# The last batch of a fused layer: one output product for both halves, and the experts' products spread over eight PSUM banks

## What is computed

```python
def _moe(x, gate_w, expert_w):
    t = x.reshape(B * S, C)
    logits = t @ gate_w.T
    w, sel = jax.lax.top_k(logits, TOP_K)                 # 2 of 8
    w = jax.nn.softmax(w, axis=1)
    comb = jnp.sum(w[..., None] * jax.nn.one_hot(sel, N_EXPERTS), axis=1)
    out = jnp.zeros_like(t)
    for e in range(N_EXPERTS):
        out = out + comb[:, e, None] * (t @ expert_w[e].T)
    return out.reshape(B, S, C)

h = x + _gqa(_rmsnorm(x, attn_norm_w), wq, wk, wv, wo)    # _gqa ends with out @ wo.T
out = h + _moe(_rmsnorm(h, ffn_norm_w), gate_w, expert_w)
```

## Time and profile before

| | us |
|---|---|
| median of 3 runs | 3667.57 |
| lowest and highest run | 3660.76, 3667.74 |
| the profiled execution's own time | 3655.43 |
| its span in the profile | 3653.7 |
| granted TensorE clock, mean over the span | 0.911 |
| TensorE busy | 3193.2 (87%) |
| VectorE busy | 2187.1 (60%) |
| ScalarE busy | 1428.5 (39%) |
| GpSimd busy | 936.6 (26%) |

### The profile page before, as it was taken

One profiled execution on the slowest core, in us unless ns is written; L12 is line 12 of the kernel. 1 busy time (PEld: TensorE's weight loads), 2 busy tenths in 40 slices (PEclk: granted clock), 3 DMA queues, 4 the chain that ended last, 5 costly groups with the idle time before them and its releaser, 6 DMA issues.

```text
span 3653.7 us, 86956 instructions
## 1 busy us (share of the span) xinstructions
PE 3193.2 (87%) x35518; PEld 2230.1 (61%) x35518; DVE 2187.1 (60%) x4820; ACT 1428.5 (39%) x3328; POOL 936.6 (26%) x851
## 2 busy tenths in 40 slices
PE   5689988888988888898868889776999999999998
PEld 5367665666666666666757767665545555554553
DVE  7566777566678666678346645635435545545444
ACT  1534443444443444344136622134433433333241
POOL 0112221412222512231406536341221231220110
PEclk7898998898998989899679989898989999999999
DMA  6111210411111301211348755384111111111000
GB/s 238 41 36 46 65 44 28 128 32 60 51 52 48 122 20 54 60 51 35 100 151 204 183 157 144 103 285 145 23 43 45 47 35 47 41 30 41 1 18 18
DMA packets 224087, 280.89 MB, mean 77 GB/s; under 512 B 35072, under 2 KB 172464, under 8 KB 223312
## 3 DMA queue, kind: packets, MB, share of 16 engines
q1 hardware_dynamic: 184448, 216.93, 18.4%
q0 software_dynamic: 34896, 54.20, 6.7%
q10 hardware_dynamic: 4352, 4.20, 0.3%
HBM read 184.64 MB, written 90.62 MB: 75 GB/s over the span
## 4 chain that ended last, share of the span: by engine, by line
PE 67%; DVE 16%; ACT 5%; issue 4%; DMA 3%; POOL 2%; DVEq 0%; ACTq 0%; SPq 0%; POOLq 0%
PE banks L3020 6%; PE banks L570 5%; DVE s_d_kq L663 4%; PE banks L2586 3%; PE banks L1936 3%; PE banks L2570 2%; PE banks L1278 2%; PE banks L806 2%; PE banks L1945 2%; PE banks L2598 2%; PE banks L966 2%; PE banks L2738 2%; PE banks L794 2%; PE banks L2828 2%; PE banks L964 2%
## 5 line engine op out<-in xcount | busy, mean ns | idle before, releaser
L570 PE MATMUL banks<-s_d_xT,s_w_qkvg 128*128 128x512 f32 x640 | 342.0, 661 | 15.9 <-DVE s_d_kq L663 11.4
L663 DVE SCALAR_TENSOR_TENSOR s_d_kq<-banks,s_conv_w,s_d_kq 128x511 f32<-128x511 f32 (+2 forms) x384 | 286.0, 745 | 49.9 <-ACT s_d_kq L615 40.3
L2700 ACT ACTIVATE s_g_pT<-banks 128x1536 f32<-128x1536 f32 (+1 forms) x96 | 152.8, 1591 | 361.0 <-PE banks L2588 361.0
L2664 DVE TENSOR_REDUCE s_g_nmax<-banks 128x4 f32<-128x512 f32 (+3 forms) x128 | 188.0, 1490 | 162.8 <-PE banks L2572 162.8
L3020 PE MATMUL banks<-s_m_we,s_m_tT 128*128 128x512 f32 x512 | 235.0, 604 | 8.1 <-DVE s_m_x L3084 7.8
L641 ACT ACTIVATE s_d_square<-banks 128x128 bf16<-128x128 f32 x512 | 134.0, 275 | 161.5 <-PE banks L599 161.5
L570 PEld LDWEIGHTS banks<-s_d_xT,s_w_qkvg 128*128 128x128 f32 x640 | 125.8, 208 | 115.8 <-issue 89.4
L615 ACT ACTIVATE s_d_kq<-banks,s_conv_w 128x512 f32<-128x512 f32 x128 | 87.8, 686 | 271.1 <-PE banks L570 270.5
L1936 PE MATMUL banks<-s_q_xsT,s_q_w 128*128 x1008 | 159.9, 282 | 38.4 <-issue 27.5
L1936 PEld LDWEIGHTS banks<-s_q_xsT,s_q_w 128*128 128x128 f32 x1008 | 153.7, 196 | 61.1 <-issue 49.1
L806 PEld LDWEIGHTS banks<-s_d_TB,s_d_XT 32*32 32x32 f32 x9216 | 111.1, 112 | 89.0 <-issue 41.9
(11 more groups left out here) (411 smaller groups left out, 7588.1 us busy)
## 6 DMA issues: line engine op xcount, KB each, us to landing
s_q_w<-w12p SPq DMA_DIRECT2D x128, 257.0 KB, 6.3
s_q_xs<-xs SPq DMA_DIRECT2D x32, 516.0 KB, 6.4
s_d_E<-sums SPq DMA_DIRECT2D x64, 256.0 KB, 3.6
s_r_xT<-xfT SPq DMA_DIRECT2D x12, 1024.0 KB
tree<-s_r_bias SPq DMA_DIRECT2D x96, 128.0 KB, 2.2
s_r_work<-xf SPq DMA_DIRECT2D x24, 512.0 KB, 4.4
og<-s_d_o SPq DMA_DIRECT2D x16, 512.0 KB, 3.0
sorted<-s_q_acc SPq DMA_DIRECT2D x32, 256.0 KB, 2.1
```

The costliest lines, as they stand in the source:

```text
L570: ins = e.matmul(bk[6 + j % 2][:], w[:, par, c, self.COL[what] + h * P:self.COL[what] + (h + 1) * P], xT[:, c, :], start=(c == 0), stop=(c ...
L663: e.scalar_tensor_tensor(d[:, a:], bk[6 + j % 2][:, 0:SEQ - a], cw[:, par, k0 + 3 - a:k0 + 4 - a], d[:, a:], ALU.mult, ALU.add).then_inc(s ...
L2664: e.tensor_reduce(self.nmax[:, t, :].rearrange("p (k d) -> p k d", k=4)[:, :, 16], psum[:, 0:4, a:a + (t + 1) * P], AX.X, ALU.max, negate= ...
L2700: e.activation(self.pT[c][:], psum[:, 0:4, 0:self.COLUMNS[c]], ACT.Exp).then_inc(self.exped, 1)
```

## The change

Two edits, both for the last batch alone.

1. In the round after the last (`m == ROUNDS`), both halves of the output product are issued together: the transposes of half 0 to bank 4 and of half 1 to bank 0, then both groups of matmuls, to banks 4 and 1. Half 1's copy goes to a part of `fT`, a tile of the linear attention that is out of use by then, instead of `aoT`. The waits that kept half 1 behind half 0 go.
2. The experts' products go to bank `2 * (k % 4) + q`, so to all eight in turn, and only from k = 3 on is there a wait for a bank. The first product (k = 0, q = 0, bank 0) is issued ahead of the logits' transposes, so ahead of the routing. VectorE's wait for the logits counts one more.

```diff
-    def half_of(self, m):
-        return (m // 4 - 1, m % 4) if m >= 4 and m % 4 < 2 else None
+    def halves_of(self, m):
+        if m == self.ROUNDS:
+            return ((m // 4 - 1, 0), (m // 4 - 1, 1))
+        return ((m // 4 - 1, m % 4),) if 4 <= m < self.ROUNDS and m % 4 < 2 else ()
+
+    def place_of(self, b, q):
+        if (b, q) == (N_BATCH - 1, 1):
+            return self.g.bank[0], self.fT[:, 0:KC, 0:256], self.g.bank[1]
+        return self.g.bank[4], self.aoT, self.g.bank[4]
...
-                if c == 2 and half:
-                    b, q = half
+                for b, q in halves if c == 2 else ():
+                    _, aoT, out = self.place_of(b, q)
                     e.wait_ge(self.e_copied, 2 * b + q + 1)
...
-                if c == 1 and half:
-                    b, q = half
-                    e.wait_ge(self.normed, 2 * min(m, R))
-                    if m > R:
-                        e.wait_ge(self.h_made, 2 * b + q)
+                for b, q in halves if c == 1 else ():
+                    into, _, _ = self.place_of(b, q)
+                    e.wait_ge(self.normed, 2 * m)
...
-                    if 2 * b + q:
+                    if 0 < 2 * b + q < 2 * N_BATCH - 1:
                         e.wait_ge(self.e_out, 2 * b + q)
...
+        if b + 1 == N_BATCH:
+            self.product_tensor(e, b, 0, 0)
         self.wait_freed(e, 0, self.before["e", b, 2][0])
         for t in range(TPB):
             ins = e.transpose(bk[0][:, t * NE:(t + 1) * NE], self.lgT[:, t * P:(t + 1) * P], g.ident[0:NE, 0:NE])
...
             for q in range(2):
-                self.wait_freed(e, q, self.before["e", b, 6 + k][q])
-                for c in range(KC):
-                    ins = e.matmul(bk[q][:], tT[:, c, t * P:(t + 1) * P], self.we[:, c, (2 * half + q) * 512:(2 * half + q + 1) * 512], start=(c == 0), stop=(c == 1))
-                ins.then_inc(self.made[q], 1)
+                if b + 1 < N_BATCH:
+                    self.wait_freed(e, q, self.before["e", b, 6 + k][q])
+                    self.product_tensor(e, b, k, q)
+                elif (k, q) != (0, 0):
+                    if k == 3:
+                        e.wait_ge(self.freed[q], self.before["e", b, 6][q])
+                    elif k > 3:
+                        e.wait_ge(self.freed[q], self.before["e", b, 2 + k][q] + 1)
+                    self.product_tensor(e, b, k, q)
+            yield
+
+    def product_bank(self, b, k, q):
+        return self.g.bank[2 * (k % 4) + q] if b + 1 == N_BATCH else self.g.bank[6 + q]
...
-        e.wait_ge(self.made[0], logits[0] + 1)
+        e.wait_ge(self.made[0], logits[0] + (2 if b + 1 == N_BATCH else 1))
...
-                e.scalar_tensor_tensor(x1[:, t, :], bk[q][:, 0:256], comb[:, t, x:x + 1], x1[:, t, :], ALU.mult, ALU.add).then_inc(me, 1)
+                e.scalar_tensor_tensor(x1[:, t, :], self.product_bank(b, k, q)[:, 0:256], comb[:, t, x:x + 1], x1[:, t, :], ALU.mult, ALU.add).then_inc(me, 1)
```

More of the change, by code:

```diff
@@ L2607, in grouped_tensor @@
         for m in range(-1, R + 2):
-            half = self.half_of(m)
+            halves = self.halves_of(m)
             for c in range(3):
@@ L2625, in grouped_tensor @@
                         for k in range(KC):
-                            ins = e.matmul(turns[:, t * 256:(t + 1) * 256], self.aoT[:, k, t * P:(t + 1) * P], self.wo[:, k, :], start=(k == 0), stop=(k == 1))
+                            ins = e.matmul(out[:, t * 256:(t + 1) * 256], aoT[:, k, t * P:(t + 1) * P], self.wo[:, k, :], start=(k == 0), stop=(k == 1))
                     ins.then_inc(self.e_out, 1)
@@ L2632, in grouped_tensor @@
                     self.values_tensor(e, m, c - 1)
-                if c == 1 and half:
-                    b, q = half
-                    e.wait_ge(self.normed, 2 * min(m, R))
-                    if m > R:
-                        e.wait_ge(self.h_made, 2 * b + q)
+                for b, q in halves if c == 1 else ():
+                    into, _, _ = self.place_of(b, q)
+                    e.wait_ge(self.normed, 2 * m)
                     for k in range(KC):
                         for t in range(2):
-                            ins = e.transpose(turns[:, k * 256 + t * P:k * 256 + (t + 1) * P], self.at[b % 2][:, 2 * q + t, k * P:(k + 1) * P], g.ident[:])
+                            ins = e.transpose(into[:, k * 256 + t * P:k * 256 + (t + 1) * P], self.at[b % 2][:, 2 * q + t, k * P:(k + 1) * P], g.ident[:])
                     ins.then_inc(self.e_turned, 1)
@@ L2643, in grouped_tensor @@
                     e.wait_ge(self.maxed, 4 * (m + 2))
-                    if half:
-                        e.wait_ge(self.h_made, 2 * half[0] + half[1] + 1)
+                    if halves:
+                        e.wait_ge(self.h_made, 2 * halves[0][0] + halves[0][1] + 1)
                     elif m >= 1:
@@ L2676, in grouped_vector @@
                 yield
-                if c == 2 and half:
-                    b, q = half
-                    h = self.h[b % 2]
+                for b, q in halves if c == 2 else ():
+                    h, (_, _, out) = self.h[b % 2], self.place_of(b, q)
                     e.wait_ge(self.xn_in, 16 * (b + 1))
                     e.wait_ge(self.e_out, 2 * b + q + 1)
-                    e.tensor_tensor(h[:, 2 * q:2 * q + 2, :], turns[:].rearrange("p (t n) -> p t n", t=2), h[:, 2 * q:2 * q + 2, :], ALU.add).then_inc(self.h_made, 1)
+                    e.tensor_tensor(h[:, 2 * q:2 * q + 2, :], out[:].rearrange("p (t n) -> p t n", t=2), h[:, 2 * q:2 * q + 2, :], ALU.add).then_inc(self.h_made, 1)
                 yield
@@ L2706, in grouped_scalar @@
                     e.activation(self.oT[:], g.bank[5][:], ACT.Copy).then_inc(self.o_out, 1)
-                if c == 1 and half:
-                    b, q = half
+                for b, q in halves if c == 1 else ():
+                    into, aoT, _ = self.place_of(b, q)
                     e.wait_ge(self.e_turned, 2 * b + q + 1)
-                    if 2 * b + q:
+                    if 0 < 2 * b + q < 2 * N_BATCH - 1:
                         e.wait_ge(self.e_out, 2 * b + q)
-                    e.activation(self.aoT[:], g.bank[4][:].rearrange("p (k n) -> p k n", k=KC), ACT.Copy).then_inc(self.e_copied, 1)
+                    e.activation(aoT[:], into[:].rearrange("p (k n) -> p k n", k=KC), ACT.Copy).then_inc(self.e_copied, 1)
                 yield
@@ L3015, in experts_tensor, with product_tensor @@
         for k in range(8):
-            t, half = k // 2, k % 2
             for q in range(2):
-                self.wait_freed(e, q, self.before["e", b, 6 + k][q])
-                for c in range(KC):
-                    ins = e.matmul(bk[q][:], tT[:, c, t * P:(t + 1) * P], self.we[:, c, (2 * half + q) * 512:(2 * half + q + 1) * 512], start=(c == 0), stop=(c == 1))
-                ins.then_inc(self.made[q], 1)
-            yield
+                if b + 1 < N_BATCH:
[7 more added lines that the diff above has]
+                    self.product_tensor(e, b, k, q)
+            yield
+    def product_bank(self, b, k, q):
+        return self.g.bank[2 * (k % 4) + q] if b + 1 == N_BATCH else self.g.bank[6 + q]
+    def product_tensor(self, e, b, k, q):
+        t, half = k // 2, k % 2
+        for c in range(KC):
+            ins = e.matmul(self.product_bank(b, k, q)[:], self.tT[:, c, t * P:(t + 1) * P], self.we[:, c, (2 * half + q) * 512:(2 * half + q + 1) * 512], start=(c == 0), stop=(c == 1))
+        ins.then_inc(self.made[q], 1)
     def experts_vector(self, e, b):
@@ L3081, in experts_vector @@
                 x = 2 * (2 * half + q)
[L3082 removed]
+                e.scalar_tensor_tensor(x1[:, t, :], self.product_bank(b, k, q)[:, 0:256], comb[:, t, x:x + 1], x1[:, t, :], ALU.mult, ALU.add).then_inc(me, 1)
                 e.wait_ge(me, pv + 22 + 2 * k + q + 1)
[L3084 removed]
+                e.scalar_tensor_tensor(x1[:, t, :], self.product_bank(b, k, q)[:, 256:512], comb[:, t, x + 1:x + 2], x1[:, t, :], ALU.mult, ALU.add).then_inc(self.freed[q], 1)
             yield
```

## The result

The change makes the kernel faster by about 0.3%, as was worked out, but from another level of times than the one it was taken from.

The account below looks back on a forecast made before the run. The prediction took the tail as two serial stretches, attention's end and routing, then a TensorE-bound one. Its terms, -2.26 - 1.35 + 0.90 - 8.66 = -11.4 us, taken from 3667.57, gave 3656.2 us, range 3648 to 3663.

Parts of the forecast that it names:

- What bounds the tail: Last 90 us: a serial stretch ending the attention, a serial stretch of routing, then a stretch bound by TensorE.
- (1): Output product's two halves issued together: half 1's sum into h starts at 3605.40 instead of 3607.66, -2.26 us.
- rival (b): First clock fall, at 3600.6 in the output product, doesn't come; gain 11.4 to 13.1 us, say 3655; chance 0.12.
- (2): Gate's product after h runs at full clock, 1.88 us instead of 3.23: -1.35 us.
- Rival (a): Gate's product stays at the low clock and delays the routing; gain 10.0 us, so 3657.5; chance 0.20.
- (3): First expert product ahead of the logits' transposes lies mostly in a wait, but delays transposes and routing by 0.90 us.
- (4): From the logits' transposes to the last combine, TensorE no longer waits for the routing: 26.35 us instead of 35.01, -8.66.
- What covers it: Combines: first at about 3618.4, VectorE needs 1.06 us for a bank, catches up with TensorE and has 3.6 us to spare.
- Rival (c): VectorE becomes the bound through slower combines or longer routing; gain 7.5 us, 3660; chance 0.05.
- Rival (e): Expert products behind the first bank's still wait for VectorE; gain under 3 us, 3665; chance 0.03.
- Rival (d): Clock swings or stays low in the run of expert products; half slow +1.5 us, all slow +14.3; chance 0.05.
- How the numbers follow: Whole kernel's time: tail's gain taken from the median of three runs, 3667.57 - 11.4 = 3656.2 us; range 3648 to 3663.

Follow-up runs that it names:

- the experts' part alone: Only the experts' products changed against the kernel before, the output product's halves still one after the other, in two profiles; ratio 0.9982 (0.9958 to 1.0006).

## Why the prediction was wrong in its range and right in its mechanism

**What bounds the tail**: right. Each link named from the chain of waits was the one that moved.

**(1) The halves**, -2.26 us: mis-sized. Half 1's sum into h starts 3603.76 - 3597.12 = 6.64 us into the tail, before it was 3607.66 - 3597.22 = 10.44: **-3.80**. Sixteen records ran in 3.73 us at full clock; the working let it fall in half 0's products, as it had before. This was rival (b), which had a chance of 0.12 and said 1.7 us more; 1.54 came.

**(2) The gate's product** at full clock, -1.35: right in size, -1.33 (3.21 to 1.88 on TensorE). Rival (a) came in none of the eight profiles with the halves together. The reason given, sixteen records that run straight through, isn't shown: in one profile of the experts' part alone the halves ran apart, with the waits of before, and the gate's product took 1.88 us as well. And what (1) and (2) took together, a first fall and then a full clock, came in no profile; that (2) was near is luck in part.

**(3) The early product**, +0.90: 1.17 by the rows (and 1.18 by the run without it), since the product and its way into the transposes took 1.91 us instead of 1.72. The routing started later by this, which cost nothing; the sum needs the term because (4) is counted from the transposes on.

**(4) No wait for the routing**, -8.66: right, -8.62 (35.01 to 3636.65 - 3610.26 = 26.39). Sum: -3.80 - 1.33 + 1.17 - 8.62 = -12.58.

**What covers it**: the first combine was at 3617.05, and VectorE took 1.11 us for a bank with a backlog, not 1.06. Spare time 3.0 us by experiment, forecast 3.6. Rival (c) didn't come but was near: with three more products ahead of the routing VectorE is the bound. Rival (e) didn't come either: no product behind the transposes waits for VectorE. Rival (d) didn't come: 60 records over eight banks ran at a clock of 1.00. The Trainium skill ("TensorE: Matmul & The Clock Gate", section "A second HAM failure mode: psum-queue depth-cycling") tells the swing of a bf16 kernel and puts it down to short idles of TensorE between groups of matmuls. The trace here has no such idle, so it doesn't contradict the page; it shows that the cycling alone doesn't bring the swing.

**The step that failed is "How the numbers follow".** The gain was taken off 3667.57, the median of three runs, and the range left it "a scatter of the runs to both sides, more downward", which came to 6.5 us below the gains of 10 to 13 and 5.5 above. Three runs don't carry that. Of the 10.6 us between 3656.2 and 3645.6, 6.8 are the level: nine runs of the same kernel have a median of 3660.76. 1.2 are the tail's gain, 12.6 instead of 11.4, from the clock in (1) less what (3) cost more. The remaining 2.6 are within the scatter of the changed kernel's own median. The level decides it: moved down by 6.8 the range is 3641 to 3656 and holds the 3645.6, moved by the 1.2 alone it doesn't. The text had the evidence: the profiled execution lay 12.1 below the median, and such an execution is drawn from the same kernel. Single executions spread over 50 us on one chip (29 runs of before, standard deviation 11.4). The mean of the four executions that were at hand was 3662.9, which less 11.4 is 3651.5; from there a range for the time had to reach at least some 10 us to each side, an estimate from the 11.4 of single executions.

## What to carry to other kernels

A serial stretch at the end of a kernel can cost an engine's idle time twice: the wait, and what a lower clock makes of the work behind it (here 3.45 us of standstill and 3.1 of low clock; behind one of 2.09 us there was none). If the work that waits needs only a place for its results, free PSUM banks are that place; count how many the chain beside it needs (here more than four) and how much spare time the reader of the banks keeps (here 3.0 us). Work out a gain against one traced execution, but before it becomes a time, ask how far executions of the same kernel lie apart: with a spread of 50 us, a gain of 12.6 us is seen to 0.04 us in the tail of a trace and only to 4 us in the means of 55 and 33 runs.

## What the runs showed of the hardware

The tail of an execution repeats to 0.04 us where the clock does the same (52.09 to 52.13 in four, 39.53 in three), while the stages ahead of it differ by 16 us and more. The same instructions at the same place may or may not lose the clock: 1.99 or 3.27 us for eight records of the output product, with waits of 0.7 to 0.8 us ahead of them in both. A fall there went with one in the gate's product, some 10 us later, in five profiles of five, and without the first the second never came. A cast on VectorE that began while GpSimd's sum was running took 0.56 and 0.57 us instead of 0.18 and ended 0.04 to 0.05 us behind it, in the two profiles in which they met. And one chip ran the whole kernel 80 us slower than the others, median against median, while in the tail the last 60 product records took 26.02 us there as elsewhere.
